# Down products finished tile by tile, an output weight rounded in unit 58, a first gate piece split ahead of a scaling, and a small product placed between two router products

## The reference

```
mod = (silu(c) @ wmod) -> sa, ca, ga, sb, cb, gb
layer 0: h = layernorm(x) * (1 + ca) + sa;  x += ga * attention(h, wq, wk, wv, wo)    # 32 heads of 16, causal
         h = layernorm(x) * (1 + cb) + sb;  x += gb * experts(h)                      # 64 experts of rank 8, the best 16
layer 1: h = layernorm(x) * (1 + ca) + sa;  x += ga * block(h)
         block: attn = (q + k + v) / 3, x1 = h + o(attn), d = down(silu(gate(x1)) * up(x1)), returns x1 + d
         h = layernorm(x) * (1 + cb) + sb;  x += gb * down(silu(gate(h)) * up(h))
```

## Time and profile before

| | us |
|---|---|
| median of 3 runs | 929.34 |
| lowest, highest | 927.82, 931.89 |
| profiled execution, its own time | 929.51 |
| its span in the trace | 927.7 |
| PE, DVE, ACT, POOL busy | 859.9, 681.3, 532.0, 192.9 |
| granted TensorE clock, mean | 0.977 of full |

### The profile page before, as it was taken

The page is one execution under the profiler, slowest core; times in us unless marked ns, Lnnn a source line. Parts: engine busy times, 40 slices in busy tenths (PEclk is TensorE's granted clock), DMA queues, the critical chain, the costliest instruction groups (busy, mean ns, idle before and its releaser), DMA issues.

```text
span 927.7 us, 13672 instructions
## 1 busy us (share of the span) xinstructions
PE 859.9 (93%) x5096; PEld 679.2 (73%) x5096; DVE 681.3 (73%) x1066; ACT 532.0 (57%) x707; POOL 192.9 (21%) x199
## 2 busy tenths in 40 slices
PE   3798999999979798998999999999988999999996
PEld 1466777777657687776888888788866888888885
DVE  3745888888879687787778786577796866667842
ACT  3412767777553544686666666576647767666820
POOL 3002566668755034100000000000120000000004
PEclk9798999999989999999999999999999999999998
DMA  9588578887750022114333333132312433332202
GB/s 312 170 251 168 54 100 136 137 129 93 152 172 1 34 69 81 46 52 138 99 105 105 106 101 114 37 101 91 114 41 69 118 104 94 99 91 77 60 1 91
DMA packets 38450, 95.35 MB, mean 103 GB/s; under 512 B 7144, under 2 KB 10216, under 8 KB 37360
## 3 DMA queue, kind: packets, MB, share of 16 engines
q1 hardware_dynamic: 34256, 89.11, 39.6%
q10 hardware_dynamic: 4128, 5.36, 1.7%
HBM read 79.56 MB, written 2.21 MB: 88 GB/s over the span
## 4 chain that ended last, share of the span: by engine, by line
PE 58%; DVE 7%; ACT 3%; issue 2%; POOL 2%; DMA 1%; POOLq 0%; SPq 0%; DVEq 0%; ACTq 0%
PE PS L1611 13%; PE PS L1613 13%; PE PS L1612 13%; PE PS L1924 5%; PE PS L1926 5%; PE PS L1925 5%; POOL X L780 2%; DVE SCR L1217 1%; DVE ST L1159 1%; DVE ACC L1232 1%; PE PS L1907 1%; PE PS L1895 1%; DVE FQ L1325 1%; PE PS L1854 1%; DMA WF<-in_LBGU 1%
## 5 line engine op out<-in xcount | busy, mean ns | idle before, releaser
L903 ACT ACTIVATE PL<-CODE 128x1024 f32<-128x1024 int32 x200 | 202.4, 1057 | 59.7 <-DVE ACC L1232 57.1
L1611 PE MATMUL PS<-HH,WRH 128*128 128x512 f32 x448 | 176.7, 394 | 11.6 <-DVE HL L1191 5.1
L1612 PE MATMUL PS<-HH,WRL 128*128 128x512 f32 x448 | 175.6, 392 | 0.0
L1613 PE MATMUL PS<-HL,WRH 128*128 128x512 f32 x448 | 175.3, 391 | 0.0
L780 POOL TENSOR_TENSOR X<-X,SCR 128x512 f32<-128x512 f32 x32 | 42.6, 1348 | 567.9 <-DVE SCR L1217 567.8
L1232 DVE SCALAR_TENSOR_TENSOR ACC<-PL,ACC 128x1024 f32<-128x1024 f32 x100 | 123.8, 1238 | 9.4 <-DVE ACC L1232 1.4
L951 ACT ACTIVATE PT<-PS 128x512 f32<-128x512 f32 x160 | 86.4, 604 | 46.4 <-PE PS L1729 25.0
L797 POOL TENSOR_TENSOR QS<-ident,MX 64x256 fp32r<-64x256 f32 x128 | 97.9, 765 | 57.5 <-DVE MX L1391 36.9
L1611 PEld LDWEIGHTS PS<-HH,WRH 128*128 128x128 f32 x448 | 84.8, 189 | 31.6 <-issue 6.3
L1613 PEld LDWEIGHTS PS<-HL,WRH 128*128 128x128 f32 x448 | 84.8, 189 | 17.9
L1612 PEld LDWEIGHTS PS<-HH,WRL 128*128 128x128 f32 x448 | 85.0, 190 | 16.8
(11 more groups left out here) (230 smaller groups left out, 1517.1 us busy)
## 6 DMA issues: line engine op xcount, KB each, us to landing
CODE<-in_CODES SPq DMA_DIRECT2D x50, 512.0 KB, 3.5
SCALE<-in_SCALES SPq DMA_DIRECT2D x100, 256.0 KB, 4.0
WM<-in_WM SPq DMA_DIRECT2D x12, 1024.0 KB, 5.6
QS<-FQ SPq DMA_DIRECT2D x32, 256.0 KB, 6.4
X<-in_X ACTq DMA_DIRECT2D x2, 1024.0 KB, 12.6
KS<-KHL SPq DMA_DIRECT2D x32, 64.0 KB, 5.3
KN<-KHL SPq DMA_DIRECT2D x32, 64.0 KB, 4.6
GAB<-gates SPq DMA_DIRECT2D x4, 512.0 KB, 3.9
```

The lines of the kernel that those rows point to most:

```text
L903: nc.scalar.activation(PL[:, n % 3], CODE[:, p % 2], ACT.Prelu, scale=scale, bias=bias, alpha=alpha).then_inc(s_plane, 1)
L1611: nc.tensor.matmul(dst, lh, rh, start=start and k == 0, stop=False)
L1612: nc.tensor.matmul(dst, ll, rh, start=False, stop=False)
L1613: ins = nc.tensor.matmul(dst, lh, rl, start=False, stop=stop and k == KC - 1)
```

## The change

Five edits. (1) `ROUND_AT` takes 57 for 58, WOH is rounded in unit 58 and no more in unit 63, and the fold of piece 5 stands behind the loop. (2) lc stands between rq 0 and rq 1 in the job list, on PE and (its halving) on DVE. (3) ACT's `deviations(1, 1)` stands ahead of the rounding of W1. (4) DVE splits piece 8, the first of gate and up, ahead of the scaling of piece 9. (5) In both down stages the last two weight chunks k = 12 and 13 are done tile by tile, both for tile 0, then both for tile 1, and so on.

```diff
-ROUND_AT = {41: 0, 46: 1, 49: 2, 54: 3, 58: 4, 61: 5, 63: 6}
+ROUND_AT = {41: 0, 46: 1, 49: 2, 54: 3, 57: 4, 61: 5, 63: 6}
...
-    for b in range(B):
-        jobs.append((("rq", b), 0))
+    jobs.append((("rq", 0), 0))
+    jobs.append((("lc",), 0))
+    jobs.append((("rq", 1), 0))
...
-            if k < MC - 1:
-                eng.wait_ge(s_hsu, (MC - 1) * n + k + 1)
+            if k < MC - 2:
+                eng.wait_ge(s_hsu, (MC - 2) * n + k + 1)
...
-                if step_at(n + 1) and step_at(n + 1)[1] == STEPS - 1:
+                if step_at(n + 1) and step_at(n + 1)[1] == STEPS - 1 and step_at(n + 1)[0] < N_QKV - 1:
                     fold(step_at(n + 1)[0])
...
-                if n == units - 1:
+                if n == units - 6:
                     act.wait_ge(s_wo, 16 * REP)
                     act.wait_ge(s_used, len(CAPS) * N_QKV)
                     nc.scalar.activation(WOH[:], WOF[:], ACT.Copy).then_inc(s_w0h, 1)
+            fold(N_QKV - 1)
             act.wait_ge(s_pv, units)
...
             norm_round(1, 0)
+            deviations(1, 1)
             for m in range(KC):
                 act.wait_ge(s_mm, J["w1", m] + 1)
                 nc.scalar.activation(W1H[:, m], PS[:, bank(("w1", m))], ACT.Copy, scale=1.0 / 3.0).then_inc(s_cast, 1)
-            deviations(1, 1)
...
             for b in range(B):
+                if b:
+                    halve(LC, ("lc",))
                 dve.wait_ge(s_mm, J["rq", b] + 1)
...
-            halve(LC, ("lc",))
...
                     if m == 1:
                         if b == 0:
                             dve.wait_ge(s_mm, J["m", KC - 1] + 1)
+                        else:
+                            split_piece(GU0)
                         scale_piece(GU0 + b)
...
-            split_piece(GU0)
             stack_low_rank(GU0 + 3)
...
+                if b == 0:
+                    pe.wait_ge(s_free, J["w1", KC - 1] + 1)
+                    pe.wait_ge(s_ll, 1)
+                    product(begin(("lc",)), lambda k: tuple(LOA[:, i, k * P:(k + 1) * P] for i in range(2)),
+                            pair(W1H, W1L, slice(0, D))).then_inc(s_mm, 1)
...
+                for k in range(MC - 2):
+                    pe.wait_ge(s_wl, ring_no(DN_START[n] + k // 2))
                     hidden_is_split(pe, n, k)
...
+                        ins = down_part(k, t)
+                    ins.then_inc(s_hsu, 1)
+                pe.wait_ge(s_wl, ring_no(DN_START[n] + MC // 2 - 1))
+                hidden_is_split(pe, n, MC - 1)
+                for t in range(NT):
+                    for k in (MC - 2, MC - 1):
+                        ins = down_part(k, t)
+                    ins.then_inc(s_mm, 1)
```

More of the change, by code:

```diff
@@ L189, in job_list @@
     norm(1, 1)
-    for b in range(B):
-        jobs.append((("rq", b), 0))
+    jobs.append((("rq", 0), 0))
+    jobs.append((("lc",), 0))
+    jobs.append((("rq", 1), 0))
     for b in range(B):
         jobs.append((("score", b), 0))
-    jobs.append((("lc",), 0))
     for i in range(NT + LAG + 1):
@@ L1803, in _ @@
                 ins.then_inc(s_mm, 1)
-            pe.wait_ge(s_free, J["w1", KC - 1] + 1)
-            pe.wait_ge(s_ll, 1)
-            product(begin(("lc",)), lambda k: tuple(LOA[:, i, k * P:(k + 1) * P] for i in range(2)),
-                    pair(W1H, W1L, slice(0, D))).then_inc(s_mm, 1)
             for i in range(NT + LAG + 1):
@@ L1910, in _, with down_part @@
                         ins.then_inc(s_x1u, 1)
-                for k in range(MC):
+                def down_part(k, t):
                     p = DN_START[n] + k // 2
-                    pe.wait_ge(s_wl, ring_no(p))
+                    w = slice(k % 2 * D, (k % 2 + 1) * D)
+                    cols = slice(t * P, (t + 1) * P)
+                    high, low = hidden_parts(n, k)
+                    hh, hl = high[:, cols], low[:, cols]
+                    if (n, k) == (1, 0):
+                        begin(("down", n, t))
+                    wh, wl = WRH[:, slot(p), w], WRL[:, slot(p), w]
+                    last = k == MC - 1
+                    nc.tensor.matmul(dst[t], hh, wh, start=(n == 1 and k == 0), stop=False, skip_group_check=True)
+                    nc.tensor.matmul(dst[t], hh, wl, start=False, stop=False, skip_group_check=True)
+                    ins = nc.tensor.matmul(dst[t], hl, wh, start=False, stop=last and n == 1, skip_group_check=True)
+                    if last and n == 0:
+                        if t == 0:
+                            pe.wait_ge(s_ldl, 1)
+                            pe.wait_ge(s_free, J["td", B - 1] + 1)
+                        nc.tensor.matmul(dst[t], TDH[:, cols], LDBH[:], start=False, stop=False, skip_group_check=True)
+                        nc.tensor.matmul(dst[t], TDL[:, cols], LDBH[:], start=False, stop=False, skip_group_check=True)
+                        ins = nc.tensor.matmul(dst[t], TDH[:, cols], LDBL[:], start=False, stop=True,
+                                               skip_group_check=True)
+                    return ins
@@ L1914, in _ @@
+                for k in range(MC - 2):
+                    pe.wait_ge(s_wl, ring_no(DN_START[n] + k // 2))
                     hidden_is_split(pe, n, k)
-                    w = slice(k % 2 * D, (k % 2 + 1) * D)
                     for t in range(NT):
-                        cols = slice(t * P, (t + 1) * P)
-                        high, low = hidden_parts(n, k)
-                        hh, hl = high[:, cols], low[:, cols]
-                        if (n, k) == (1, 0):
-                            begin(("down", n, t))
-                        wh, wl = WRH[:, slot(p), w], WRL[:, slot(p), w]
-                        last = k == MC - 1
-                        nc.tensor.matmul(dst[t], hh, wh, start=(n == 1 and k == 0), stop=False, skip_group_check=True)
-                        nc.tensor.matmul(dst[t], hh, wl, start=False, stop=False, skip_group_check=True)
-                        ins = nc.tensor.matmul(dst[t], hl, wh, start=False, stop=last and n == 1, skip_group_check=True)
-                        if last and n == 0:
-                            if t == 0:
-                                pe.wait_ge(s_ldl, 1)
-                                pe.wait_ge(s_free, J["td", B - 1] + 1)
-                            nc.tensor.matmul(dst[t], TDH[:, cols], LDBH[:], start=False, stop=False,
-                                             skip_group_check=True)
-                            nc.tensor.matmul(dst[t], TDL[:, cols], LDBH[:], start=False, stop=False,
-                                             skip_group_check=True)
-                            ins = nc.tensor.matmul(dst[t], TDH[:, cols], LDBL[:], start=False, stop=True,
-                                                   skip_group_check=True)
-                        if last:
-                            ins.then_inc(s_mm, 1)
@@ L1939, in _ @@
-                    if not last:
-                        ins.then_inc(s_hsu, 1)
+                        ins = down_part(k, t)
[6 more added lines that the diff above has]
+                    ins.then_inc(s_mm, 1)
                 if n == 0:
```

## The result

The changed kernel takes 919.94 us (median of 4 runs, 918.86 to 921.20); the kernel before, on the same chip, 928.58 (4 runs, 927.46 to 931.89). The ratio is 0.990, 95% interval 0.988 to 0.992: 8.6 us faster by the medians, 9.4 by the ratio, about 1%. The forecast was 916.0, with a range of 912 to 920.5. In the two profiled executions the difference is larger, 929.51 to 918.86, that is 10.65; the forecast's sum was 13.3. Executions of one kernel differ by 1 to 8 us, so I compare traces stage by stage, and medians only by their ratios.

The account below looks back on a forecast made before the run. TensorE, busy 93% of the span, was taken to bound the kernel, with five places where it or its chain waits. Terms 3.9 + 3.6 + 3.5 + 2.0 + 0.3 = 13.3 off 929.5 gave 916.2, rounded down to 916.0; range 912 to 920.5.

Parts of the forecast that it names:

- rival B: Attention edit gives nothing; the wait for WOF, lower clock and DVE being held take it all: 919.8, chance 0.12.
- The end: Second down stage tile by tile: POOL keeps up with PE, so the last addition ends 3.9 us earlier.
- WOH in unit 58: Behind the attention: DVE's 4.83 wait for WOH goes, wo 4 starts earlier; 3.6 us, in 1.5 to 5.6.
- lower clock: In the attention: PE, after standing some 2.3 at unit 59, may run at half speed, costing up to 2.5 us.
- the hold: Behind the attention: a two-SBUF-input DVE operation stands until POOL's ATL split ends; gain 4.0 to 4.7, not 5.6.
- lc and the square root: Router: lc fills PE's 2.98 wait before rq 1, normalising starts earlier; 3.5 us, in 2.3 to 4.1.
- Piece 8 first: Gate and up: splitting piece 8 first removes PE's 4.67 wait; 2.0 us gained, in 0.5 to 5.3.
- Slack there: Behind chunk 7: HID is ready 3.1 us before PE needs it; less the 1.14 split, 2.0 remains.
- the ring: Gate and up: scaling, low-rank load, rounding and stacking turn once per chunk; 0.5 gain if its transfers get slower.
- my sign of being wrong: Gate and up: the forecast is wrong if PE's wait for HID comes back in every chunk.
- The first down stage: First down stage tile by tile: DVE could gate earlier; 0.3 us, in -0.3 to 1.
- C: Gains hidden: PE, ahead, waits for pieces from decoding; only 3.9 and less than 1 elsewhere remain: 925, chance 0.05.

Follow-up runs that it names:

- e7: The changed kernel with the rounding of WO put back to the last unit and the fold of piece 5 back in the loop: 922.80 us, ratio 0.9920.
- e11: The changed kernel with both down stages chunk by chunk again, as before: 923.63 us, ratio 0.9933.
- e6: The changed kernel with POOL's split of AT moved behind its first four additions of wo: 919.02 us, ratio 0.9881.
- e12: The changed kernel with lc behind the scores, its halving behind the selection and batch 1's square root behind W1's roundings again: 922.41 us, ratio 0.9936.
- e4: The kernel before with only the split of piece 8 moved first: 930.67 us, ratio 1.0009.
- e1: The changed kernel with piece 8 split behind the x1 loop again, as before: 917.79 us, ratio 0.9887.

## Why the prediction was right, and where it wasn't

The time lies in the range, 0.6 below its upper end, because four of five terms held and the fourth did not. By the number alone it fits rival B (919.8) better than the forecast (916.0). What rules B out is not the time but the traces, in which the attention's edit gives 3.6, and e7.

1. **The end, 3.9.** The trace gives 3.9 (8.8 to 4.9 in E), for the reason given: POOL, which needs 1.24 for a tile, keeps up with one each 1.36. e11 gives the same 3.9.
2. **WOH in unit 58, 3.6.** The pair of traces gives 3.59 at wo 4, and the means over eleven traces 3.6 too. Most steps stood where I had put them: WOF landed at 252.6 (252.4 forecast), division and AT met at 274.3 (273.0 forecast), the last split took 4.32. ACT waited 3.27, where I had said some 2.4. The lower clock that I had only feared did come in this pair: 1.6 of the 21.7 behind WOH. It is the larger part of A's spread with the edit (29.1 to 32.8), up to 2.8 against up to 1.2 from the landing of WOF (8.9 to 10.1 behind the first issue). What I had wrong is the weight of the hold. I let it set wo 4; on PE's path it cost 0.63 to 0.75, not 2. And I let DVE's chain carry the gain, where PE got it by not standing ahead of wo 0: 1.6 from the earlier start and 2.0 from the full clock behind it. That the sum of 3.6 is met so closely is in part luck. The Trainium skill's rule (SBUF — State Buffer, section "SBUF: two separate sides"), a lock for the whole instruction, is borne out by this row: the split of heads ends at 279.98, 0.5 behind POOL's split of AT. Beside DVE operations with two SBUF inputs the same section names those in a 2-port mode as taking the lock. No row here shows the mode of the normalising operations; that e6 has them held, 6.03 against 1.92, agrees with it. I had weighed only two-input operations when I wrote its expectation.
3. **lc and the square root, 3.5.** 3.9 in the pair of traces, 3.5 if B of before and of e7 are compared, 4.8 by e12. The steps held: rq 1 waits 0.28, and no half clock behind it. Some 1.3 of the 3.5 are the half clock of before, which e4's execution didn't have and e12's had for longer.
4. **Piece 8 first, 2.0: the step that failed.** In the pair of traces the lead shrank from 7.5 ahead of the stage to 6.2 at its last HID: a loss of 1.3 instead of a gain of 2.0, and below my lower bound of 0.5. The step in the prediction was "Slack there: ... That is 3.1; less the 1.14 ..., 2.0". I read a slack at one chunk and took it for a stock that the edit could spend. It was PE's lateness against a ring that ran on its own. The first HID comes from the ring, not from PE: 96.1 behind the first FL in the kernel before, 96.8 in the changed one, though PE was 6 ahead. And once PE is no longer late, the ring's turn counts in every chunk, 11.85 against PE's 11.4; PE waited for HID in three more chunks. In every one would have been my sign of being wrong. I had named the ring and said "0.5 if the ring's transfers get slower", but never added up one turn. The timeline of the kernel before held all that it takes: scaling 1.22, SP 1.1, the load some 4, BST, WRH and fold 2.5, SG and HID 1.3, split 1.2, some 11.3 without any wait.
5. **The first down stage, 0.3.** 0.6 by D in the pair, 0.5 by e11.

The sum: 3.9 + 3.6 + 3.9 - 1.3 + 0.6 = 10.7, the difference of the profiled executions (10.65). Put back one by one on the clock, the terms give 3.4 (1 and 5), 2.2 (2), 3.7 (3) by ratios against the mean of the changed kernel's two, 0.9896, and piece 8 -0.8: 8.5, where the whole change gives 9.7 by the same ratios and 8.6 by the medians. Each has an uncertainty of 2 us or more. None of the rivals came true as written. C had the right place (PE, ahead, waits) with the wrong engine's work: it was one load's landing and not the decoding.

What stays open: why the landing of the low-rank load is a little longer in the changed kernel than before. The tile's loads in the stage (who waited, in all and times; then issue to landing, us), before and after:

```profile
  ACT BST L1028: 14.6, 10
...
DMA to landing us min/median/max: 3.6/3.7/4.6
```

```profile
  ACT BST L1029: 16.4, 9
...
DMA to landing us min/median/max: 3.6/4.0/4.9
```

ACT's wait is 1.46 a turn before and 1.82 after, and these 0.36 are the whole difference of the turns (nine of them, 434.61 to 538.22 before: 11.51 each; 11.85 after). In e1, where piece 8 is split behind, the median is 4.0 as well, which speaks against the order of the split as the cause. Other executions may fall otherwise; nothing was run for it. Nor does any run tell what decides how long the half clock behind one and the same wait lasts.

## What to carry to other kernels

Before giving an engine a head start, add up one full turn of the loop that feeds it, DMA issue and landing included; if the turn is longer than that engine's own work, the head start is spent in waits and nothing comes out at the end. SP's list, worked off in order, puts every load behind the waits of those ahead of it: a load whose own condition was met 6 us earlier belongs ahead of one that waits for late work. When two edits each measure as nothing, try them together: here one removed PE's lateness and the other the ring's, and only both gave the 4 us. And before pricing a hold, see what the engine on the path is doing meanwhile: 3.6 us of a held DVE were 0.75 us for PE.

## What the runs showed of the hardware

A hold between POOL and DVE doesn't end with moving POOL's instruction; it falls on the next DVE operation of a kind that can be held. Beside POOL's split of AT (4.6 alone) a split of heads with two SBUF inputs took 4.32 instead of 0.69. A normalising operation with one SBUF input took 2.7 instead of 0.53 beside the last 2.4 of the same split; the four of them, beside this and two short instructions of POOL, took 6.03 instead of 1.92. Beside short instructions of POOL of 1.3 to 1.5 such an operation took up to 1.5. Not held beside the split of AT in e6: gating from PSUM, 0.69, and the statistics, which read SBUF alone, 0.69. Cutting POOL's 4.6 into four of 1.3 to 1.7 brought the split of heads to 1.00 and the four normalising operations to 4.31. The split of WO took 3.23 beside POOL's split of AT and 2.29 alone. That is the price list that I would use for such an overlap.

One and the same stand of PE was not followed by the same clock in each execution. Behind 3.0 between rq 0 and rq 1 the granted clock was 0.80 over 2.2 us and 0.50 over the next 2.2 in the kernel before, 0.50 over the 6 us from 308 to 314 in e12, and 1.00 in e4. Against e4 that cost 1.3 us in the kernel before and 2.4 in e12.
